# Building the sorted edge list of a graph layer with indirect transfers instead of one-hot products, and moving a stream of weight transfers from POOL to ScalarE

## What is computed

```
def _rgcn(x, edge_index, edge_type, weight, root, bias):
    src, dst = (edge_index[0], edge_index[1])
    msgs = x[src]
    out = x @ root + bias
    for r in range(weight.shape[0]):
        mask = (edge_type == r).astype(x.dtype)
        sums = jax.ops.segment_sum(msgs * mask[:, None], dst, num_segments=n)
        cnt = jax.ops.segment_sum(mask, dst, num_segments=n)
        mean = sums / jnp.maximum(cnt, 1.0)[:, None]
        out = out + mean @ weight[r]
    return out
u = _rgcn(x, edge_index, edge_type, weight, root, bias)
z = jnp.concatenate([u, x], axis=1) @ w_gate + b_gate
h = jnp.tanh(u) * z + x * (1.0 - z)
```

## Time and profile before

| what | value |
|---|---|
| median of the three runs | 1782.47 us (1781.53 to 1783.1) |
| the profiled execution, its own time | 1785.86 us |
| its span | 1784.1 us |
| PE busy | 1701.7 us, 95% |
| DVE busy | 1098.0 us, 62% |
| ACT busy | 727.1 us, 41% |
| POOL busy | 766.3 us, 43% |

### The profile page before, as it was taken

The page is one execution under the profiler, slowest core; times in us unless marked ns, Lnnn a source line. Parts: engine busy times, 40 slices in busy tenths (PEclk is TensorE's granted clock), DMA queues, the critical chain, the costliest instruction groups (busy, mean ns, idle before and its releaser), DMA issues. The chain is left out here.

```text
span 1784.1 us, 22190 instructions
## 1 busy us (share of the span) xinstructions
PE 1701.7 (95%) x7896; PEld 1407.2 (79%) x7896; DVE 1098.0 (62%) x1484; ACT 727.1 (41%) x1231; POOL 766.3 (43%) x662
## 2 busy tenths in 40 slices
PE   7999999999999999999999999999889978999996
PEld 5888888888888888888877887878678866787885
DVE  8554666564564243334489999999889887434300
ACT  2315566541331312122166665665521213454453
POOL 1002222215765555601256656555355423555532
PEclk9999999999999999999999999999989977999998
DMA  5336655557234434343598888888745446786753
GB/s 209 95 113 209 189 169 171 176 156 254 84 99 126 141 118 149 113 144 129 186 352 307 299 290 294 282 270 299 265 169 171 166 141 214 191 234 171 179 106 59
DMA packets 140715, 333.94 MB, mean 187 GB/s; under 512 B 19234, under 2 KB 35666, under 8 KB 140608
## 3 DMA queue, kind: packets, MB, share of 16 engines
q0 software_dynamic: 50816, 159.29, 29.4%
q1 hardware_dynamic: 89792, 173.23, 29.0%
HBM read 236.07 MB, written 96.39 MB: 186 GB/s over the span
## 5 line engine op out<-in xcount | busy, mean ns | idle before, releaser
L1402 POOL DMA_INDIRECT gathered<-Y,edge_row x184 | 231.5, 1258 | 183.9 <-PE banks L1571 142.4
L835 ACT ACTIVATE ghi<-gathered,edge_w 128x1024 fp32r<-128x1024 f32 x184 | 211.0, 1151 | 141.6 <-DMA gathered<-Y,edge_row 87.6
L1378 POOL DMA_INDIRECT edge_w<-INV,edge_key x184 | 208.6, 1133 | 119.1 <-DMA edge_w<-INV,edge_key 96.7
L1429 PE MATMUL banks<-whi,xhi 128*128 128x512 f32 x640 | 252.7, 395 | 0.6 <-DVE xlo L1024 0.6
L1201 DVE SCALAR_TENSOR_TENSOR glo<-gathered,edge_w,ghi 128x1024 fp32r<-128x1024 f32 x184 | 235.7, 1281 | 26.4 <-ACT ghi L835 26.0
L1431 PE MATMUL banks<-whi,xlo 128*128 128x512 f32 x640 | 249.8, 390 | 0.0
L1430 PE MATMUL banks<-wlo,xhi 128*128 128x512 f32 x640 | 249.7, 390 | 0.0
L1570 PE MATMUL banks<-ghi,sel 128*128 128x512 f32 x368 | 146.2, 397 | 11.9 <-DVE glo L1201 11.7
L785 ACT ACTIVATE ring_hi<-raw_chunk 128x512 fp32r<-128x512 f32 x112 | 66.5, 624 | 207.5 <-PE banks L1533 152.3
L1571 PE MATMUL banks<-glo,sel 128*128 128x512 f32 x368 | 144.3, 392 | 0.0
L1429 PEld LDWEIGHTS banks<-whi,xhi 128*128 128x128 f32 x640 | 120.6, 188 | 25.3 <-DVE xlo L1024 1.2
(11 more groups left out here) (338 smaller groups left out, 3690.2 us busy)
## 6 DMA issues: line engine op xcount, KB each, us to landing
raw<-in_L_ffn_w SPq DMA_DIRECT2D x24, 1024.0 KB, 10.0
Y<-y_out SPq DMA_DIRECT2D x80, 256.0 KB, 3.3
t_set<-in_L_gnn_weight POOLq DMA_DIRECT2D x64, 256.0 KB, 4.8
TW<-t_set POOLq DMA_DIRECT2D x64, 256.0 KB, 3.8
raw_chunk<-TW SPq DMA_DIRECT2D x64, 256.0 KB, 2.8
w_stage<-in_L_gnn_weight SPq DMA_DIRECT2D x30, 512.0 KB, 5.1
raw_chunk<-in_L_gnn_weight SPq DMA_DIRECT2D x48, 256.0 KB, 2.9
Y<-half_v SPq DMA_DIRECT2D x40, 256.0 KB, 2.2
```

The lines of the kernel that those rows point to most:

```text
L835: nc.scalar.activation(ghi[:, t % HR], gath[t % GR][:], ACT.Copy, scale=edge_w[:, t:t + 1]).then_inc(g_hi, 1)
L1378: nc.gpsimd.indirect_dma_start(out=edge_w[:, t:t + 1], out_offset=None, in_=INV, in_offset=bass.IndirectOffsetOnAxis(ap=edge_key[:, t:t + ...
L1402: nc.gpsimd.indirect_dma_start(out=gath[t % GR][:], out_offset=None, in_=Y, in_offset=bass.IndirectOffsetOnAxis(ap=edge_row[:, t:t + 1], a ...
L1429: pe.matmul(psum[slot][:], xhi[:, k, at], whi[h][:, k], start=(k == 0), stop=False)
```

## The change

It has five parts.

1. PE's matmuls into PLACE_BANK, DVE's one-hots `oh_val` and `oh_lo`, and ACT's `values` are gone. DVE instead works out one place number for each edge (`place_at`), and POOL writes the pair of values of each edge to that row of a table SORTED in DRAM: first the table is cleared by one transfer, then 167 indirect transfers, one for each column of edges and two in flight, and then one transfer reads the list back into `placed`. The matmuls into COUNT_BANK stay.
2. `t_load` and `t_store` are issued by ACT (`t_turn`), between its copies and roundings of relations 1 to 3.
3. DVE works out the keys after its first three chunks, late in relation 3, behind a wait for the list (`list_moved`).
4. DVE's chunks 3 to 5 stand ahead of the first sum of x; before, the sums began first.
5. ACT's `sum_hi` of the first two sums no longer stands at tiles 3 and 6 of relation 3's second half but in Strassen's product 0, behind the copies of tiles 0 and 3; those of the other two stand behind the copies of tiles 1 and 2 of product 1.

```diff
 def columns(r, part, first=False, last=False):          # PE
     pe.wait_ge(cols_ready, (r - 1) * SG1 + part + 1)
-    pe.wait_ge(vals_ready, (r - 1) * SG1 + part + 1)
-    for i in range(CPQ):
-        pe.matmul(PLACE_BANK[:, 0:2 * ET], oh_lo[:, i], oh_val[:, i].rearrange("p a t -> p (a t)"), ...)
     for i in range(CPQ):
         ins = pe.matmul(COUNT_BANK[:, 0:BT], oh_klo[:, i], oh_khi[:, i], ...)
...
+pool.wait_ge(places_ready, 1)                           # POOL
+pool.dma_start(SORTED[0:P * ET, :].rearrange("(p t) a -> p t a", t=ET), placed[:]).then_inc(list_moved, 16)
+pool.wait_ge(list_moved, 16)
+for c in range(EFULL + (EREST > 0)):
+    if c >= 2:
+        pool.wait_ge(w_gathered[c % 2], 16 * (c // 2))
+    nc.gpsimd.indirect_dma_start(
+        out=SORTED, out_offset=bass.IndirectOffsetOnAxis(ap=place_at[:, c:c + 1], axis=0),
+        in_=pair[:, c], in_offset=None).then_inc(w_gathered[c % 2], 16)
+for i in range(2):
+    pool.wait_ge(w_gathered[i], 16 * LISTED[i])
+pool.dma_start(placed[:], SORTED[0:P * ET, :].rearrange("(p t) a -> p t a", t=ET)).then_inc(list_moved, 16)
 pool.wait_ge(inv_ready, 1)
 pool.dma_start(INV.rearrange("(a b) c -> a (b c)", b=BT), inv[:]).then_inc(inv_out, 16)
...
+def t_turn(m):                                          # ACT
+    t_store(m - 1)
+    if m + 1 < T_STEPS:
+        t_load(m + 1)
...
 if last and h == 1:                                     # ACT, relation 3
-    if j in (3, 6):
-        sum_hi((3, 6).index(j))
     if j < 8:
         chunk_hi(j)
...
+SUM_AT = ((0, 0), (0, 3), (1, 1), (1, 2))               # ACT, Strassen's products
-        if n == 0 and i in (2, 4):
-            sum_hi(i // 2 + 1)
+        if (n, i) in SUM_AT:
+            sum_hi(SUM_AT.index((n, i)))
...
+for c in range(raw_n):                                  # DVE
+    chunk_lo(c)
+dve.wait_ge(list_moved, 32)
+... (the keys, as they were)
+for c in range(raw_n, raw_n + 3):
+    chunk_lo(c)
 for i in range(TS):
     dve.wait_ge(t_moved[i], t_stored[i])
 dve.wait_ge(inv_out, 16)
 step(both(s4sum, a21h, a21l, ALU.add))
 step(both(s4sum, s4sum, a22h, ALU.add))
 step(both(s4sum, s4sum, a22l, ALU.add))
-chunk_lo(0)
 step(both(s2sum, s4sum, a11h, ALU.subtract))
 both(s2sum, s2sum, a11l, ALU.subtract).then_inc(s_raw, 1)
-chunk_lo(1)
-chunk_lo(2)
+chunk_lo(6)
 less_hi(0, s2hi, s2lo, s2sum)
-chunk_lo(3)
+chunk_lo(7)
```

More of the change, by code:

```diff
@@ L760, in relation, with t_time, t_load, t_store @@
                                 for part in range(1, SG1):
[L761 to L776 removed]
+                                    if t_time(part) == h * NT + j + 1:
+                                        t_turn((r - 1) * SG1 + part)
+                            if last and h == 0 and j < 9:
+                                t_turn(SORT_R * SG1 + j)
+                def t_time(part):
+                    return (part * 2 * NT * 10 // SG1 + 4) // 10
+                def t_load(m):
+                    if m >= TS:
+                        act.wait_ge(t_moved[m % TS], 16 + 64 * (m // TS))
+                    s, k, part = m // 8, m // 2 % KH, m % 2
+                    for a in range(2):
+                        rows_of = weight[R0 + s][a * HALF + k * P:a * HALF + (k + 1) * P, :]
+                        act.dma_start(t_set[:, m % TS, a], rows_of.rearrange("p (b n) -> p b n", b=2)
+                                      [:, :, part * TQ:(part + 1) * TQ]).then_inc(t_moved[m % TS], 16)
+                def t_store(m):
+                    s, k, part = m // 8, m // 2 % KH, m % 2
+                    act.wait_ge(t_made, 4 * m + 4)
+                    for a in range(2):
+                        at = s * D + a * HALF + k * P
+                        act.dma_start(TW[at:at + P, :].rearrange("p (b n) -> p b n", b=2)
+                                      [:, :, part * TQ:(part + 1) * TQ], t_set[:, m % TS, a]).then_inc(t_moved[m % TS], 16)
+                def t_turn(m):
+                    t_store(m - 1)
+                    if m + 1 < T_STEPS:
+                        t_load(m + 1)
                 def chunk_hi(c):
@@ L1344, in _ @@
                                    vec[EFULL * P:E].rearrange("(p c) -> p c", c=1)).then_inc(edges_in, 16)
-                def t_load(m):
-                    if m >= TS:
-                        pool.wait_ge(t_moved[m % TS], 64 * (m // TS))
-                    s, k, part = m // 8, m // 2 % KH, m % 2
-                    for a in range(2):
-                        rows_of = weight[R0 + s][a * HALF + k * P:a * HALF + (k + 1) * P, :]
-                        pool.dma_start(t_set[:, m % TS, a], rows_of.rearrange("p (b n) -> p b n", b=2)
-                                       [:, :, part * TQ:(part + 1) * TQ]).then_inc(t_moved[m % TS], 16)
@@ L1440, in columns @@
                     pe.wait_ge(cols_ready, (r - 1) * SG1 + part + 1)
-                    pe.wait_ge(vals_ready, (r - 1) * SG1 + part + 1)
-                    for i in range(CPQ):
-                        pe.matmul(PLACE_BANK[:, 0:2 * ET], oh_lo[:, i], oh_val[:, i].rearrange("p a t -> p (a t)"),
-                                  start=first and i == 0, stop=last and i == CPQ - 1, skip_group_check=True)
                     for i in range(CPQ):
```

109 lines of the change are left out of this document (44 added, 65 removed).

## The result

The changed kernel takes 1801.11 us (median of 4, 1796.46 to 1802.36) against 1782.0 us for the kernel before in the same session (4 runs, 1778.63 to 1783.1). The ratio is 1.0108 with a 95% interval of 1.0095 to 1.012: slower by 19 us, where 6.6 us faster was forecast. The profiled execution has a span of 1800.6 us and its own time of 1802.36 us.

A forecast was written before the change was run, and what follows sets the result against it. PE was taken to bound the kernel, without a gap up to 880 us. Terms -28.3 + 21.0 + 0.7 = -6.6 us took the median from 1782.5 to 1775.9 us, range 1752 to 1812.

The forecast's parts named there:

- The matmuls that leave PE: Relations 1 to 3 on PE: seven placing matmuls gone from each of 24 parts, 1.18 us each part, 28.3 us saved.
- The hand-over: Strassen's product 2 on PE: it waits for low chunks behind the later sums, which gives back 21.0 us.
- the chain from s2hi to that chunk: Sum steps on ACT and DVE, from s2hi at 474.2 to product 2's first low chunk at 516.0.
- the clock term: PE behind the wait at product 2: work at the lower 1.2 GHz clock costs 0.7 us, bounds 0 and 2.
- The list: POOL's clear, 167 indirect writes and read back: ready at 416, 34 us early, so it costs nothing.
- The rule for a late list: DVE's keys before s2hi: list wanted by 450.2; each microsecond later is a microsecond on PE.
- p: Period of POOL's 167 indirect writes: taken as 1.75 us, from gathers; up to 1.95 would cost nothing.
- the formula: Time at which POOL has the list read back: 124 + 167 p, in us.
- The first rival: List late, period above 1.95 us, before DVE's keys: 1812 us at 2.17, 1898 at 2.68; chance 0.24.
- break-even of 1.99: Write period in us at which the list is 6.6 us late; beyond it the kernel gets slower.
- The row that the text set aside: Experts' result, indirect write of 4 KB rows: lands in 7.8 against a gather's 6.0, giving a period of 2.68.
- At no cost: ACT's weight-sum issues, about 0.33 us each, and POOL's later edge_w gathers, covered by 61.9 us idle: nothing.

The follow-up runs named there:

- e3_four_order: Kernel of e2, but keys, chunk remainders, sums and the sums' copies stand where the kernel before has them: 1749.99 us, ratio 0.9819.
- e2: Kernel of e1_pads with four indirect writes in flight where there were two: 1774.16 us, ratio 0.9957.
- e4: Kernel before, with only the order of keys, chunks, sums and the sums' copies moved as in the change: 1803.47 us, ratio 1.0117.
- e1_pads: Changed kernel, with the 126 padding edges written to 126 different rows where all went to one: 1780.12 us, ratio 0.9989.
- e8: Changed kernel again for a second profile, with one more wait on POOL (already passed by VectorE) ahead of the list: 1798.06 us, ratio 1.0103.
- e5: Kernel before, with only the weight-sum transfers issued by ScalarE instead of POOL: 1781.9 us, ratio 1.0008.
- e7: Changed kernel, with the padding on two rows, 62 and 64 writes, where all went to one: 1791.25 us, ratio 1.0056.
- e10: Kernel of e3_four_order, but with all 126 padding edges on one row again: 1919.26 us, ratio 1.0773.

## Why the prediction was wrong

- **The matmuls that leave PE, 28.3 us: right.** Relation 2 ends at 361.8 where it ended at 390.1, and e3_four_order keeps the whole gain to the last Strassen matmul.
- **The hand-over, 21.0 us: right.** It measured 21.4 (e2 against e3) and 21.5 (e4 against before). PE waits 18.7 us at product 2 in e2 and e4, as worked out (498.0 against 516.7), and the chain from s2hi to that chunk took 41.8 us for 41.8. With the clock term the forecast was 21.7. PE's waits are 18.9 us in e2; the other 2.5 us pass while PE is busy at a granted clock of 0.50 (517 to 521 us) and 0.89 (to 523), the lower level that the clock term expected.
- **The list, 0 us: this step failed.** "I take 1.75" and "about 6 us for the last landing and the read back" gave a list at 416. The period was 2.015 us, which alone makes (2.015 - 1.75) x 167 = 44 us, and the last landing and the read back took 26 us (452.63 to 478.79), of which POOL waited 21.08 for the landing, 18 more than with spread padding. Together they made the keys start at 478.8, where 450.2 was the latest that costs nothing.
- **The rule for a late list: right.** Keys were wanted to end 7.7 us behind 450.2, at 457.9. In the changed kernel they start at 478.8 for 450.2, 28.6 us late, and its last Strassen matmul stands 900.9 - 872.5 = 28.4 us behind that of e2_four, whose list is in time. e1_pads, with p near 2.0 and spread padding, is at 882.6, +10.1 us; the formula gives 124 + 167 x 2.0 = 458, 8 us late. So the step splits into 10.1 us for the period and 18.3 us for the padding. By the second profile, whose list was issued 3 us sooner (e8, 896.0), the padding's part is 13.4.
- **The sum by measured terms:** -28.3 + 21.4 + 10.1 + 18.3 = +21.5 us at the end of the Strassen part, which is 900.9 - 879.4. The end of the kernel shows 16.5 us in the two profiles and 19.1 in the medians: the stage of the gathered rows takes 384.8 us after (905.3 to 1290.1) and 389.4 before. It was 385.1 in e5 as well, whose median is that of the kernel before, so no gain follows from it. The two profiles with the longer stage, before and e4 (389.8), are of executions 3.9 and 2.9 us above their medians; why stayed open.
- **The first rival was the right one,** the late list, with the right exchange of a microsecond for a microsecond. It got 0.24 with p = 2.17 or 2.68. The period of 2.0 was inside its bounds and just past its break-even of 1.99. The padding was not in the text at all, though the diff has it: one constant multiplies all padding positions.
- **Why the price of a write was wrong:** more the traffic beside it than the kind of transfer. The 1.75 came from gathers at a DMA share of 0.28 to 0.48. Of the 167 writes 142 started before 420 us, beside a share of 0.60 to 0.76, and the trace of the kernel before has 0.58 there (136 to 362 us). At a share of 0.72 a gather takes the same 2.14 us as a write (e3), and behind 420 us, at 0.20, a write takes 1.32, less than any of the three stretches of gathers in the earlier trace rows. The store of INV, at 2.6 us, is one transfer.
- **The row that the text set aside,** a write that lands 1.8 us after a gather, would have been too dear: p = 2.68 is further from 2.015 than 1.75 is, and the landing is 3.3 us in the median (e1) for 4.6 by that row. Only the busiest stretch comes near it, with 2.35 us a write and a landing of 4.0.
- By the Trainium skill's rule that spoke against this part (DMA: Bandwidth & Descriptors, Specifications and Anatomy), an 8 byte write into HBM would land later than a 4 byte gather into SBUF. The traces do not agree: a write lands in 2.1 us where little else moves (e1 behind 420 us), and the fastest gather of the kernel before in 2.2; over the list the writes' median is 3.3 us for 2.8 of the gathers, but beside heavier traffic.
- **At no cost,** as forecast: ScalarE's issues (e5), and the gathers of edge_w, which ended at 817, with 29.7 us of idle time still before the bias load.

## What to carry to other kernels

A transfer that many steps in a row depend on is priced by its landing beside the traffic of that very stretch, and by how many are in flight; while it is unknown, more in flight is the cheap way out: here four cost two more semaphores and took the list off the path. Look where padding goes: 126 writes of one instruction to one address cost some 18 us here, and a row for each lane of padding costs two short instructions. When a result is made in another place, ask separately what the new order of the consumers costs: here the order moved to cover a late list cost 21 us, and with four in flight it was not needed, for 1750 us and 1.8% less than the kernel before.

## What the runs showed of the hardware that was not expected

- 126 writes of 8 bytes to one address took 16.5 to 18 us longer to land than 126 to as many addresses (e8 and the first profile against e1), 64 some 6 us longer (e7).
- An indirect write of 128 pieces was issued every 1.27 us at best, and landed in a time that grew with the traffic of other queues: in e1 a median of 2.1 us at a DMA share of 0.19 and 4.0 at 0.76. An indirect gather went at the same 2.14 us each as a write beside like traffic (0.72 and 0.70).
- A transfer of 256 KB as two blocks a lane costs ScalarE 0.58 us (store) and 0.83 us (load) to issue, up to 2.06, where SyncE issues a store of y in 0.32.
- In one loading PE started a matmul only every 2.80 us, with no wait of the program between them, while indirect writes went on at 1.27 us each and all queues together moved 1 GB/s (e10). It cost 166 us; the same kernel elsewhere took 1753 and 1757 us, and the kernel before took 1782.15 on that chip. The cause stays open: no run parts chip from loading. Whoever times such a kernel should do so on more than one chip.
